# Sixteen instead of fifteen of a batch's 32 output products on GpSimd, new engine orders, and a rearranged set-up

## What is computed

```python
def step(h, xs):
    dA_t, dBu_t, C_t = xs
    h = dA_t * h + dBu_t
    y = jnp.einsum('ben,bn->be', h, C_t)
    return (h, y)
...
y1 = act_mx * z1                     # z1: scan forwards, z2: scan of the flipped sequence
out = jnp.einsum('bse,de->bsd', y1 + y2, Wf) + bf + skip
return x + gate[:, None, :] * out
```

## Time and profile before

| | us |
|---|---|
| median of three executions | 4430.05 |
| the profiled execution's own time | 4430.37 |
| its span on the core | 4428.6 |
| VectorE (DVE) busy | 4050.2 |
| GpSimd (POOL) busy | 3849.4 |
| TensorE (PE) busy | 3722.4 |
| ScalarE (ACT) busy | 3609.1 |
| mean granted TensorE clock, share of full | 0.942 |

### The profile page before, as it was taken

How to read it: one execution, slowest core, us unless ns; L and a number is a source line. 1 busy time by engine, 2 the same in 40 slices (tenths; PEclk the granted TensorE clock), 3 DMA queues, 4 the chain that set the end, 5 groups by cost and what they waited for, 6 DMA issues and landing times.

```text
span 4428.6 us, 74058 instructions
## 1 busy us (share of the span) xinstructions
PE 3722.4 (84%) x26464; PEld 2478.3 (56%) x26464; DVE 4050.2 (91%) x5619; ACT 3609.1 (81%) x8678; POOL 3849.4 (87%) x1772
## 2 busy tenths in 40 slices
PE   5988888889888888888888888888888888888664
PEld 3665555556565555555555555555655555556432
DVE  4449999989999999999999999999999999999995
ACT  0368878878988899889888998898888988988763
POOL 0019988989999999999999999999999999999994
PEclk6899999989999999999999999999999999999876
DMA  4033444543444445434444444344444444444541
GB/s 122 11 75 91 94 105 95 118 113 82 117 117 114 109 113 120 111 91 112 117 117 112 110 117 117 91 106 117 117 114 107 117 117 103 94 117 114 123 107 32
DMA packets 334160, 462.12 MB, mean 104 GB/s; under 512 B 56204, under 2 KB 165847, under 8 KB 333789
## 3 DMA queue, kind: packets, MB, share of 16 engines
q1 hardware_dynamic: 333632, 457.32, 43.7%
q10 hardware_dynamic: 158, 0.08, 0.0%
HBM read 370.26 MB, written 86.50 MB: 103 GB/s over the span
## 4 chain that ended last, share of the span: by engine, by line
ACT 28%; DVE 18%; PE 18%; POOL 7%; issue 5%; DMA 2%; SPq 0%; POOLq 0%; ACTq 0%; DVEq 0%
ACT ps L706 11%; PE ps L171 10%; DVE ps L721 5%; POOL S_X L767 5%; ACT A_ring L472 3%; DVE A_sm L429 3%; DVE S_X L721 3%; PE ps L804 3%; DVE S_X L736 2%; POOL S_X L780 2%; PE ps L376 2%; ACT C_xh L154 1%; PE ps L545 1%; ACT T_v L303 1%; DVE C_dd L579 1%
## 5 line engine op out<-in xcount | busy, mean ns | idle before, releaser
L767 POOL TENSOR_TENSOR S_X<-S_slot,S_bc 128x1024 f32<-128x1024 f32 x1024 | 2403.2, 2366 | 174.8 <-PE ps L804 119.2
L706 ACT ACTIVATE ps<-S_slot,acol 128x256 f32<-128x256 f32 x4096 | 1742.7, 468 | 190.5 <-DVE S_X L736 180.8
L721 DVE TENSOR_TENSOR_SCAN ps<-ps,S_X 128x512 f32<-128x512 f32 x1088 | 1300.0, 1214 | 37.4 <-POOL S_X L767 19.6
L780 POOL TENSOR_TENSOR S_X<-S_X,S_bc 128x1024 f32<-128x1024 f32 x480 | 1132.6, 2366 | 38.7 <-DVE S_X L721 32.6
L721 DVE TENSOR_TENSOR_SCAN S_X<-ps,S_X 128x512 f32<-128x512 f32 x960 | 1141.2, 1208 | 16.3 <-ACT ps L706 13.7
L736 DVE TENSOR_TENSOR S_X<-ps,S_bc 128x512 f32<-128x512 f32 x1088 | 712.5, 675 | 5.7 <-issue 0.2
L804 PE MATMUL ps<-S_X,sum 128*32 128x256 f32 x8192 | 615.6, 403 | 102.6 <-POOL S_X L780 62.4
L804 PEld LDWEIGHTS ps<-S_X,sum 128*32 128x32 f32 x8192 | 198.9, 112 | 388.8 <-issue 169.2
L429 DVE TENSOR_REDUCE A_sm<-ps 128x4 f32<-128x1024 f32 x256 | 311.0, 1215 | 62.7 <-PE ps L376 59.5
L376 PE MATMUL ps<-A_kP,A_qP 32*128 32x256 f32 x2048 | 292.7, 403 | 45.5 <-DVE A_sm L429 31.4
L395 PE MATMUL ps<-A_qP,A_kP 32*128 32x256 f32 x2048 | 296.7, 407 | 21.6 <-ACT A_ring L472 15.2
(11 more groups left out here) (295 smaller groups left out, 6882.0 us busy)
## 6 DMA issues: line engine op xcount, KB each, us to landing
S_slot<-scr_dd SPq DMA_DIRECT2D x1024, 256.0 KB, 4.7
scr_dd<-C_dd SPq DMA_DIRECT2D x64, 1024.0 KB, 5.3
S_bc<-scr_bc SPq DMA_DIRECT2D x256, 256.0 KB, 6.3
L_xin<-in_x SPq DMA_DIRECT2D x32, 256.0 KB
scr_x<-A_x SPq DMA_DIRECT2D x32, 256.0 KB, 5.8
T_x<-scr_x SPq DMA_DIRECT2D x32, 256.0 KB
out_x<-xs SPq DMA_DIRECT2D x32, 256.0 KB, 6.1
T_gate<-scr_gate SPq DMA_DIRECT2D x32, 128.0 KB
```

What stands on the lines that cost most here:

```text
L706: ins = a.activation(B["bank"][half_at(b, u, i)][:, n * T:(n + 1) * T], B["slot"][:, s, j, 0, :], ACT.Exp, scale=K.k["acol"][:, s, LINES * ...
L721: v.tensor_tensor_scan(line(x if u in ON_POOL else decay), line(decay), line(x), 0.0, ALU.mult, ALU.add).then_inc(S.scan.sem, 1)
L767: g.tensor_tensor(B["X"][:, u % RING], B["slot"][:, s, :, 1, :], rep(B["bc"][:, s, q, :], 1, LINES), ALU.mult).then_inc(S.b.sem, 1)
L780: g.tensor_tensor(B["X"][:, u % RING], B["X"][:, u % RING], rep(B["bc"][:, s, NQ + q, :], 1, LINES), ALU.mult).then_inc(S.cp.sem, 1)
```

## The change

- `ON_POOL` takes in unit 31: 16 output products on GpSimd, 16 on VectorE.
- All strings of `FIRST` and `TURN` are new.
- Set-up: SP issues from the start, without the wait for VectorE; 16 loads (masks, condition, FiLM) go on ScalarE's queue ahead of its other work; the first state-space weights are a stage "ada" of their own, on SP behind "attention". The 18 scalings by the norm's scale go from VectorE to ScalarE. The bias memsets, the mask conversion and the mask split stand ahead of the attention evictions on VectorE; the bias row's split stands ahead of layer 1's FiLM evictions. The bias row's transfers go from ScalarE's queue to SP's, behind all its loads. Eight of the nine memsets ahead of the main block move into the set-up, and so does batch 0's input load. `pcol` is stored last, and its landing is waited for by batch 0's first transfers (`K.W.columns`) instead of by the block.
- Waits: nobody but VectorE waits for `K.ready` ahead of the program; TensorE waits for layer 0's constants (`land["a"]`) ahead of the key product; ScalarE waits once for `vA`'s column of ones.

The diff, cut to its core:

```diff
-ON_POOL = frozenset(range(1, UNITS - 1, 2))
+ON_POOL = frozenset(range(1, UNITS, 2))
...
     p.wait_ge(S.dve.sem, S.dve.at(b, "qsub"))
+    if L == "L0":
+        p.wait_ge(K.land["a"].sem, K.land["a"].at(b))
...
+    if b == 0:
+        a.wait_ge(K.ready, 2)
...
-    v.wait_ge(K.land["a"].sem, K.land["a"].at(b))
+    v.wait_ge(K.land["xin"].sem, K.land["xin"].at(b))
...
-    q.dma_start(B["xin"][:], K.x_in[b].rearrange("(t p) d -> p t d", p=P)).then_inc(K.land["a"].sem, 16)
+        q.dma_start(B["xin"][:], K.x_in[b].rearrange("(t p) d -> p t d", p=P)).then_inc(K.land["xin"].sem, 16)
+    else:
+        q.wait_ge(K.W.columns, 16)
...
-LOADS = {"attention": 31, "conditions": 21, "scans": 21}
+LOADS = {"attention": 31, "masks": 3, "conditions": 13, "ada": 5, "scans": 21}
...
         @block.vector
...
+            mark["padded"] = t.n
+            where = k["bias"][0:2 * PARTS, sections["L1k"]]
+            t.count(t.ready().memset(k["bias"][:], 0.0))
...
+            for om in K.omL:
+                t.count(t.ready().memset(om[:], 0.0))
+                t.count(t.ready().memset(om[0:PARTS, :], 1.0))
+            t.count(t.ready().memset(K.dbc[ONE:ONE + 1, :], 1.0))
...
+            t.ready().wait_ge(got["masks"], 16 * LOADS["masks"])
...
+            split(lambda i: M["mparts"][:, :, i, :], mr[:], M["mback"][:])
+            mark["mparts"] = t.n
             t.ready().wait_ge(got["attention"], 16 * LOADS["attention"])
             for L in ATTENTION:
                 for m in "qkv":
                     padded = L == "L1" and m != "v"
-                    for i in range(KD):
-                        dst, src = k[L + "w" + m][:, i, :], M[L + m + "raw"][:, i, :]
-                        t.count(t.ready().tensor_scalar(padded_heads(dst) if padded else dst, heads(src) if padded else src, M[L + "g"][:, i:i + 1], None, ALU.mult))
...
             for L, (_, _, _, _, at) in FILM.items():
-                if L == "L3":
-                    split(lambda i: M["mparts"][:, :, i, :], mr[:], M["mback"][:])
-                    mark["mparts"] = t.n
+                if L == "L1":
+                    v.wait_ge(round1, 16)
+                    split(lambda i: M["bparts"][:, i, :], M["rowsb"][:], M["back"][:])
+                    mark["bparts"] = t.n
...
-            t.ready()
+            t.ready().wait_ge(got["ada"], 16 * LOADS["ada"])
...
         @block.scalar
...
+                load(a, "masks", M["mi"][:], W["mask_BxS_ik0"])
...
+                load(a, "conditions", M["cond"][:], W["cond_2048"])
...
+                for L in FILM:
+                    load(a, "conditions", M[L + "fw"][:], tiles("%s_cond_%s" % (L, FILM[L][0])))
             a.preload_act_table_set(ACT_SET)
+            a.wait_ge(vector, mark["padded"])
+            a.wait_ge(got["attention"], 16 * LOADS["attention"])
+            for L in ATTENTION:
+                for m in "qkv":
...
+                        t.count(a.activation(padded_heads(dst) if padded else dst, heads(src) if padded else src, ACT.Copy, scale=M[L + "g"][:, i:i + 1]))
+            a.wait_ge(vector, mark["mparts"])
             a.wait_ge(got["conditions"], 16 * LOADS["conditions"])
...
-            t.ready().wait_ge(vector, mark["allb"])
-            a.dma_start(scr["bias"].rearrange("(a n) -> a n", a=1), M["allb"][:]).then_inc(round3, 16)
...
         @block.sync
...
-                q.wait_ge(vector, 12)
...
+                q.dma_start(K.xin[:], K.x_in[0].rearrange("(t p) d -> p t d", p=P)).then_inc(K.land["xin"].sem, 16)
...
             assert asked == LOADS, asked
+            q.wait_ge(vector, mark["allb"])
+            q.dma_start(scr["bias"].rearrange("(a n) -> a n", a=1), M["allb"][:]).then_inc(round3, 16)
+            q.wait_ge(round3, 16)
+            q.dma_start(M["rowsb"][:], scr["bias"].rearrange("(a n) -> a n", n=P)).then_inc(round1, 16)
             q.wait_ge(vector, mark["mparts"])
             q.dma_start(scr["mask"], M["mparts"][:]).then_inc(stored, 16)
+            q.wait_ge(vector, mark["bparts"])
+            q.dma_start(scr["bparts"].rearrange("i (a n) -> a i n", n=P), M["bparts"][:]).then_inc(round2, 16)
+            q.wait_ge(round2, 16)
+            q.dma_start(k["bias"][0:PARTS, :], scr["bparts"]).then_inc(stored, 16)
             q.wait_ge(vector, mark["pcol"])
-            q.dma_start(scr["pcol"].rearrange("b p n -> p b n"), M["pcol"][:]).then_inc(stored, 16)
-            q.wait_ge(stored, 16 * 3)
+            q.dma_start(scr["pcol"].rearrange("b p n -> p b n"), M["pcol"]).then_inc(K.W.columns, 16)
+            q.wait_ge(stored, 16 * 2)
...
-    "Pool": "SSCPSSSSSSSPPPSSSCSPSPSSPSPSSSPSTSPPSSSPSASPSPSCSPSLS",
+    "Pool": "SLPSSCSPSSSSPPSSSPSSSSPCSPSPSSPSSSPSTSPSSPSPSASPSPCSSP",
...
-                for om in (K.L["omL0"], K.A["omL1"], K.T["omL3"]):
-                    v.memset(om[:], 0.0).then_inc(K.ready, 1)
-                v.memset(K.C["dbc"][ONE:ONE + 1, :], 1.0).then_inc(K.ready, 1)
-                v.wait_ge(K.ready, 5)
+                v.wait_ge(K.ready, 1)
...
-                p.wait_ge(K.ready, 9)
```

More of the change, by code:

```diff
@@ L1069, in setup_weights, with load @@
         made, vector, scalar, masks = sem("set_pe"), sem("set_dve"), sem("set_act"), sem("set_pool")
-        got = dict(K.W.got, attention=sem("set_ld_attention"), conditions=sem("set_ld_conditions"))
+        got = dict(K.W.got, **{n: sem("set_ld_" + n) for n in ("attention", "masks", "conditions", "ada")})
         round1, round2, round3, stored = sem("set_round1"), sem("set_round2"), sem("set_round3"), sem("set_stored")
-        mark = {}
+        mark, asked = {}, {}
+        def load(e, stage, dst, src):
+            e.dma_start(dst, src).then_inc(got[stage], 16)
+            asked[stage] = asked.get(stage, 0) + 1
         block = ctx.enter_context(nc.Block())
@@ L1226, in _ @@
-            a.wait_ge(round2, 16)
-            a.dma_start(k["bias"][0:PARTS, :], scr["bparts"]).then_inc(stored, 16)
+            t.ready()
         @block.sync
         def _(q):
-            asked = {}
-            def load(stage, dst, src):
-                q.dma_start(dst, src).then_inc(got[stage], 16)
-                asked[stage] = asked.get(stage, 0) + 1
             with nc.allow_non_contiguous_dma(reason="columns of bias vectors, once"):
-                q.wait_ge(vector, 12)
                 for L, ns in ATTENTION.items():
@@ L1240, in _ @@
                     a = ["%s_cond_%s" % (L, n) for n in ns]
-                    load("attention", M[L + "g"][:], cols(a[0]))
-                    load("attention", M[L + "b"][:], cols(a[1]))
+                    load(q, "attention", M[L + "g"][:], cols(a[0]))
+                    load(q, "attention", M[L + "b"][:], cols(a[1]))
                     for n, m in ((2, "q"), (4, "k"), (6, "v")):
-                        load("attention", M[L + m + "raw"][:], tiles(a[n]))
-                        load("attention", M["L1%sb" % m][:] if L == "L1" and m != "v" else M["allb"][0:1, sections[L + m]], line(a[n + 1]))
@@ new lines, in _ @@
+                        load(q, "attention", M["L1%sb" % m][:] if L == "L1" and m != "v" else M["allb"][0:1, sections[L + m]], line(a[n + 1]))
+                    load(q, "attention", k[L + "wo"][:], tiles(a[8]))
+                    load(q, "attention", M["allb"][0:1, sections[L + "o"]], line(a[9]))
+                load(q, "attention", M["allb"][0:1, sections["wf"]], line("L2_cond_bf"))
+                q.dma_start(K.xin[:], K.x_in[0].rearrange("(t p) d -> p t d", p=P)).then_inc(K.land["xin"].sem, 16)
@@ L1276, in _ @@
-                    load("scans", M["dp"][:, s, :], cols("L2_cond_Dp" + m))
-                    load("scans", M["al" + n][:], tiles("L2_cond_Alog" + m))
+                    load(q, "scans", M["wc" + n][:], tiles("L2_cond_Wc" + m))
+                    load(q, "scans", M["wd" + n][:], W["L2_cond_Wdbc" + m])
+                    load(q, "scans", M["wdt" + n][:], tiles("L2_cond_Wdt" + m))
+                    load(q, "scans", M["bc" + n][:], cols("L2_cond_bc" + m))
+                    load(q, "scans", k["wdt"][ONE:ONE + 1, s, :], line("L2_cond_bdt" + m))
@@ L1294, in __init__ @@
         self.pe, self.dve, self.act = sem("W_pe"), sem("W_dve"), sem("W_act")
-        self.got, self.stored, self.spread = {"scans": sem("W_ld")}, sem("W_stored"), sem("W_rows")
+        self.got, self.stored, self.columns, self.spread = {"scans": sem("W_ld")}, sem("W_stored"), sem("W_columns"), sem("W_rows")
         self.mark, self.names = {}, products_of_scans()
@@ L1690, in _ @@
             def _(g):
-                g.wait_ge(K.ready, 9)
                 program(g, K, "Pool")
@@ L1695, in _ @@
             def _(q):
-                q.wait_ge(K.ready, 9)
                 program(q, K, "SP")
```

159 lines of the change are left out of this document (70 added, 89 removed).

## The result

The changed kernel takes 4400.33 us (median of four executions, 4395.94 to 4403.39) against 4431.6 for the kernel before on the same chip (4429.83 to 4439.83): ratio 0.9925, interval 0.9908 to 0.9942, so 0.75% faster. Forecast were 4384 and 4345 to 4416. The range held it, the point lay 16 us too low, and the parts were further off than the sum. The profiled execution took 4395.94, its span 4394.2; the parts are read against the span of before, 4428.6. That is the fastest of the four, so the parts add up to 34.4 us where the medians are 31.3 apart.

A forecast was written before the change was run, and what follows sets the result against it. VectorE was taken to bound the kernel, with 2.6 us idle a batch. 4430.4 - 16 (set-up) - 28 (middle) - 6 (start-up order) + 4 (tail) - 0.3 = 4384 us, range 4345 to 4416.

The forecast's parts named there:

- Faster by more than 0.2%: Whole kernel: faster by more than the 0.2%, 9 us, that a measurement can tell from no change; chance 0.88.
- Change 1, the middle: Batches from 1052 to 4152 us: unit 31's product to GpSimd shortens the period by 1.15, 28 us in all, ends 0 and 50.
- If VectorE keeps its 2.6 us of idle, the period is 122.2 + 2.6: Middle: VectorE's work falls to 122.2 us a batch, its idle stays, so the period is 124.9 instead of 126.04.
- the relief isn't passed on: Middle: two engines at 97 to 98% in fixed lists keep the period at 126; 4418 us, chance 0.20.
- The slower rival: GpSimd becomes the bound, product 31 at each batch's end lengthening the period by 2.32 to 128.4; 4486 us, chance 0.05.
- Change 2, start-up order: About the first five batches: the relief of 1.15 a batch gives 6 us, ends 10 lost and 25 won.
- Change 3, the set-up: Set-up before layer 0: earlier loads and barrier save 16 us, bounds -24 and -8.
- my 68: Set-up: the barrier, and with it TensorE's first block-two work, comes near 68 us instead of 80.7.
- near 57: Set-up: the path of attention weights, scalings, sigmoid and three FiLM stages ends near 57 us, next if SP's loads ended early.
- My low bound's condition: Set-up: only -8 us if the two queues slow each other and the attention weights come late.
- Change 4, the tail: From 4152 us on: GpSimd's extra product in batch 30 costs 2.3 and unit 31's second product 1.6, together +4 us.
- The signs I named: Traces: period 124.9, first load before 1.5; wrong if scan waits exceed 3, bias leaves before 40, first S_X product not 16 earlier.

The follow-up runs named there:

- three cuts of the split kernel: Split kernel with gate product on one chunk of four, direction 1's dt*u likewise, or three of eight maxima over half the keys: 4375.68, 4366.96, 4380.06 us.
- split kernel: Changed kernel with each S_bc load split in two, the B half issued right behind the slot load: 4379.24 us, ratio 0.9894 to the kernel before.
- the move alone: Kernel before with only unit 31's product moved to GpSimd, its letters moved in the old lists: 4544.42 us, ratio 1.0264.
- orders alone: Kernel before with ON_POOL, FIRST and TURN of the changed kernel, set-up untouched: 4423.81 us, ratio 0.9999.
- the run that has it alone: Changed kernel's set-up with ON_POOL, FIRST and TURN of the kernel before: 4401.98 us, ratio 0.9944.

## Why the prediction was right or wrong

- **Faster by more than 0.2%**: right, and the range held, the size in part by luck. Two gains were sized too small, by 9 and 14.5 us, and the third, of 28, was a loss of 7.6; the first two made good two thirds of the third. Against the spans that leaves -34.4 for a forecast of -46. The median lies 4.4 us above the profiled execution, which makes up most of the rest of the 16.
- **Change 1, the middle: wrong.** The step that failed is "If VectorE keeps its 2.6 us of idle, the period is 122.2 + 2.6". I took the engine nearest to full for the bound. The period is the length of the longest closed chain through several engines. The kernel before's chain that ended last had 28% on ScalarE and only 18% on VectorE, and that was on the page I read. Relief on VectorE counts only where its piece lies on that chain and no other chain nearly as long stands next to it. Measured: -28 forecast, +7.6 happened, 126.07 to 126.40 a batch. The rival "the relief isn't passed on" described the middle. Its mechanism, two full engines that hand stalls to each other, was only half of it: VectorE's 1.2 us did become stalls, but the three cuts of the split kernel show that neither engine's fullness sets the time. Of the period that the kernel after has, 0.8 us was the detour over the `S_bc` load.
- **The slower rival** had the wrong place. "A product more at the batch's end" costs when the lists aren't planned anew: 4.5 us a batch with the old ones, at the one place tried, twice the 2.32 I gave it. With the new orders the move is bearable, and they bring the detour over the `S_bc` load.
- By the Trainium skill, GPSIMD Engine Reference, section Engine selection, elementwise work on a tile belongs on VectorE, GpSimd being about twice as slow with two inputs. The traces come near that (2368 ns against two of 676, 1.75 times), and the move alone, 2.6% slower, agrees with its advice; but with the new lists the period followed neither engine's total.
- **Change 2, start-up order: mis-sized.** -6 forecast, -20.5 measured (orders alone: from +3.6 at batch 0 to -19.1 at batch 4), inside its ends of -25 and +10. I sized it by the relief of one product, 1.15 a batch, though VectorE had 10 us of idle there that a new order can take.
- **Change 3, the set-up: mis-sized.** -16 forecast, -25.1 at the first gate, -21.5 in the run that has it alone. TensorE's second block began at 60.05, 8 us earlier than my 68. The bias row's last transfer was issued at 53.02, not 63.3, so the round trips were not the bound; the FiLM path, which I had "near 57", set the end at 59.17. My low bound's condition, "the attention weights come late", was met (25.12, not 17 to 20), and still the sum was too small.
- **Change 4, the tail: right.** +4 forecast, +3.5 measured; GpSimd works 125.88 of 126 us between 4152 and 4278.
- **The signs I named:** first load at 0.80 (below 1.5), ring waits gone, GpSimd's waits for scans 66.8 us in 23.7 batches, 2.8 each (below 3), bias at 43.99 (above 40), GpSimd's last product ending at 4339.22, 2.4 us after the last scan. But the period was not 124.9, and GpSimd's first scan input came 28.8 us earlier, not 16: two signs of the forecast being wrong in its parts.

## What to carry to other kernels

In a software pipeline with fixed lists on every engine, find the closed chain: follow the chain of waits until it comes back to the same piece a period later, and test it by adding work on it and beside it. Only relief on that chain shortens the period, and only down to the next chain; here that was 0.3 us away for a piece on GpSimd and 0.04 for one on VectorE. Lengthening is not symmetric to it: 1.7 us on the engine with 15 us to spare cost 1.7 where it met the chain. So a move between engines is judged by where both pieces stand to the chain, and a planned schedule is better improved by looking for a transfer on it, as the split of the B rows did.

## What the runs showed of the hardware

- Busy time hides relief. VectorE lost products worth 1.18 us a batch from start to start and its busy time fell by 0.3 (123.44 of 126.04 us in the batch from 2506.46 of the kernel before, 123.10 of 125.58 in the split kernel). Neighbouring instructions overlap when nothing is waited for: in the split kernel a maximum of 1.23 us at 2481.35 is followed by the next instruction after 1.14 us, and a scan of 1.21 us at 2477.31, behind which VectorE waits 0.31, after 1.52. That this makes up the difference is argued, not shown.
- A second load queue took from the first: issued 7.2 us sooner beside 3 MB on the other queue, the attention weights landed 1.1 us later (25.12 against 24.00); with those 3 MB behind them, at 16.44. Both together moved more, 304 GB/s from 5 to 20 us in the split kernel against 258 from 5 to 16 with those loads behind, and the DMA engines were busy throughout in both (share 1.06 and 1.07).
- The same product of 32 matmuls of 128x32 took 4.77, 5.86 and 7.03 us in three kernels, the last at a granted clock of 0.50. In the split kernel the clock fell inside this product, while TensorE was busy without a break from 37.93: granted 1.00 from 39 to 40, 0.73 from 40 to 41, 0.50 from 41 to 42.
- The first gate of kernels with the same set-up and start-up lists lies between 417.40 and 429.66 us in the profiled executions of eight kernels, so single marks there are good to some 6 us.
